# p in three bf16 parts read by TensorE at register addresses, and more rows fetched singly

## The chip, the cores and the metric

The kernel runs on one core of a Trainium2 chip. A core has five engines with a queue of instructions each: TensorE (PE in the profile, its weight loads PEld), VectorE (DVE), ScalarE (ACT), GpSimd (POOL) and SyncE (SP); SP, ACT and POOL also issue DMAs. The metric is the device time of one execution in microseconds.

## The reference

One layer of graph attention over 6250 nodes with 128 features and 206,250 edges (src, dst), then ELU, a residual and a layer norm:

```python
recv, send = edge_index[:, 0], edge_index[:, 1]
n_in, n_out = node[recv], node[send]
wn_out = n_out @ W_lin + b_lin
e_ij = leaky_relu2(jnp.concatenate([n_in, n_out], axis=-1) @ W_att + b_att)
a_ij = (e_ij @ w_alpha)[:, 0]
seg_max = jax.ops.segment_max(a_ij, recv, num_segments=N_NODES)
a_exp = jnp.exp(a_ij - seg_max[recv])
denom = jax.ops.segment_sum(a_exp, recv, num_segments=N_NODES)
alpha = a_exp / jnp.maximum(denom[recv], 1e-12)
n_i = jax.ops.segment_sum(alpha[:, None] * wn_out, recv, num_segments=N_NODES)
x = _layernorm(x + elu(n_i), axis=-1)
```

The product with W_att splits into a part p of the receiver and a part q of the sender, so p, q and v = wn_out are computed once per node and not once per edge.

## The kernel before

**Table.** 49 blocks of 128 nodes are taken in 25 pairs. For each pair PE computes p, q and v (`project`, L921 the f32 product and L922 the bias), ACT copies p into SBUF (`p_all`, L700, f32) and q and v into an outgoing tile (L704), and SP stores the latter to the table `qv_table` in DRAM, one row of 1 KB per node. Before every other pair PE transposes the next x (L910) and ACT copies it (L695). There are two PSUM buffers, so a projection waits for the copies of the pair two before it.

**Sort.** Meanwhile DVE sorts the first set of edges by receiver's block, a bitonic network (L1185, L1186) in runs; between runs PE transposes the keys (L942) and ACT copies them back (L715, L721, L722). Three lists set where on PE and ACT the pairs stand among the runs: `TABLE_BEFORE` ahead of the first turn, `TABLE_BEHIND` (run: pairs) and `TABLE_LAST`.

**Main loop.** The sorted edges are 1660 units of 128 edges, in 415 chunks of 4 units, in four sets; the next set is sorted inside the loop of the one before (same lines). For chunk k:
- POOL gathers q and v of the senders of each unit with one indirect DMA (L666) into a ring of 8 chunks. Every 11th chunk (`ROW_CHUNKS`) has one unit that is not gathered: its 128 rows are fetched by one DMA each, spread over the 11 chunks before, 104 issued by SP (L584) and 24 (`BY_ACT`) by ACT (L810, in `fetch_rows`), with addresses loaded into registers 8 at a time.
- DVE compares each edge's receiver lane with the lanes' numbers: `onehotT` (L1574).
- ACT loads four block numbers packed in a word into its registers (L443) and copies the four blocks of p that the units need to `p_unit` at register addresses (L761, `stage_p`).
- PE, `hidden`: for each unit it transposes the gathered q (L1005) and adds p_unit x onehotT in PSUM (L1007, f32, which takes two passes).
- ACT makes the slope (L768), DVE the leaky relu (L1581), PE the logits with a mask per block (L1017, L1018), DVE the chunk's lows and running peaks (L1588, L1603) and the growth (L1613).
- ACT `weigh` takes four exps (L778), PE transposes the weights (L1025), ACT copies them (L793, `copy_weights`) and turns growth into a shrink factor (L787, `lessen`); PE sums weights x v per unit (L1033) and DVE adds it to the node sums (L1625).

The order in each engine's queue is written out by hand. ACT's step k is weigh(k+2), slope(k+4), copy_weights(k+1), lessen(k+2), stage_p(k+6), fetch_rows(k+6), then side work, such as a count of edges per block in chunks 23 to 71 (L869). PE's is high_sums(k), hidden(k+4), turn_weights(k+1), mask(k+3), low_sums(k+1). Before its loop ACT fetches the rows of the first `ROWS_AHEAD` = 6 chunks.

Of the kernel before, what the change touches and what calls it, by code (L numbers as in the profile page):

```python
# [13 lines left out]
P = 128  # L14
# [6 lines left out]
def gnn_kernel(nc, x, src, dst, w_lin, b_lin, w_att, b_att, w_alpha, out):  # L21
# [83 lines left out]
    ROWS_EACH = 8  # L105
    ROW_CHUNKS = 11
    BY_ACT = 3 * ROWS_EACH
    BY_SP = UNIT - BY_ACT
# [80 lines left out]
    with ExitStack() as ctx:  # L189
        def sb(name, shape, dt):  # L190
            return ctx.enter_context(nc.sbuf_tensor(name, shape, dt))
# [4 lines left out]
        def sem(name):  # L196
            return ctx.enter_context(nc.semaphore(name))
# [18 lines left out]
        pad_rows = sb("pad_rows", [P, R], F32)  # L216
        p_all = sb("p_all", [P, NB * F], F32)
        p_unit = sb("p_unit", [P, 2, CHUNK], F32)
        sums = sb("sums", [P, NB, F + 1], F32)
# [109 lines left out]
        kept_i = kept[:].bitcast(I32)  # L329
        onehotT_b = onehotT[:].bitcast(BF16).rearrange("p r (e h) -> p r e h", h=2)[:, :, :, 1]  # L330
        columns_i = columns[:].bitcast(I32)
# [57 lines left out]
        pqv_ps = sem("pqv_ps")  # L389
        p_ready = sem("p_ready")  # L390
        p_staged = sem("p_staged")
        qv_ready = sem("qv_ready")
# [284 lines left out]
        def _(act):  # L677
# [12 lines left out]
            def copy_xT(q):  # L690
# [4 lines left out]
                a.activation(xT[:, q % 2, 0:n], masked_ps[:, q % 2, 0:n], ACT.Copy).then_inc(xT_ready, 1)  # L695

            def table_pair(g):
                n = min(2, NB - 2 * g)
                act.wait_ge(pqv_ps, g + 1)
                a.activation(p_all[:, 2 * g * F:(2 * g + n) * F].rearrange("p (n f) -> p n f", f=F),  # L700
                             pair_ps[g % 2][:, 0:n, 0:F], ACT.Copy).then_inc(p_ready, 1)
                if g >= 2:
                    act.wait_ge(qv_stored[g % 2], g // 2 * 16)
                a.activation(qv_out[:, g % 2, 0:n, :], pair_ps[g % 2][:, 0:n, F:3 * F], ACT.Copy).then_inc(qv_ready, 1)  # L704
                if g % 2 == 0 and g // 2 + 1 < QUADS:
                    copy_xT(g // 2 + 1)

            copy_xT(0)
            for g in TABLE_BEFORE:
# [39 lines left out]
            for g in TABLE_LAST:  # L749
                table_pair(g)  # L750

            def stage_p(k):

                s, n = place(k)
                if n == 0:
                    act.wait_ge(blk_packed, 4 * (s + 1))
                of = blocks_of(mybir.EngineType.Activation, k, F)
                if k >= 2:
                    act.wait_ge(hidden_done, k - 1)
# [56 lines left out]
            act.wait_ge(pad_rows_stored, 16)  # L816
            act.wait_ge(p_ready, PAIRS)
            for k in range(2):
                stage_p(k)
            for k in range(ROWS_AHEAD):  # L820
                fetch_rows(k)
            for k in range(4):
                if k >= 2:
                    weigh(k - 2)
                slope(k)
                stage_p(k + 2)
                if k >= 2:
                    lessen(k - 2)
            copy_weights(0)

            def step(k):
                if k + 2 < NCH:
                    weigh(k + 2)
                if k + 4 < NCH:
                    slope(k + 4)
                if k + 1 < NCH:
                    copy_weights(k + 1)
                if k + 2 < NCH:
                    lessen(k + 2)
                if k + 6 < NCH:  # L840
                    stage_p(k + 6)
                fetch_rows(k + ROWS_AHEAD)
                besides(k)
# [54 lines left out]
        def _(pe):  # L898
# [26 lines left out]
            def table_pair(g):  # L925
                if g % 2 == 0 and g // 2 + 1 < QUADS:
                    turn_x(g // 2 + 1)
                if g + 1 < PAIRS:
                    project(g + 1)

            turn_x(0)
            project(0)
# [60 lines left out]
            def hidden(k):  # L993

                pe.wait_ge(onehotT_ready, k + 1)
                pe.wait_ge(p_staged, k + 1)
                if k >= 2:
                    pe.wait_ge(leaky_ready, k - 1)
                pe.wait_ge(gathered[k % U], come[k])
                if k in single_no:  # L1000
                    pe.wait_ge(*fetched_in(single_no[k]))
                whole = hidden_ps[:, k % 2, :]
                for c in range(C):
                    unit = slice(c * P, (c + 1) * P)
                    t.matmul(whole[:, unit], rows_at_unit(k, c)[:, 0:F], identf[:], is_transpose=True,  # L1005
                             start=True, stop=False, skip_group_check=True)
                    mm = t.matmul(whole[:, unit], p_unit[:, k % 2, unit], onehotT[:, k % 4, unit],  # L1007
                                  start=False, stop=True, skip_group_check=True)
                mm.then_inc(hidden_done, 1)

            def mask(k):

                pe.wait_ge(leaky_ready, k + 1)
                if k >= 2:
                    pe.wait_ge(weightsT_ready, k - 1)
                whole = masked_ps[:, k % 2, :]
                t.matmul(whole, other[:], onehotT_b[:, k % 4, :], start=True, stop=False)  # L1017
                t.matmul(whole, w_cols[:], leaky[:, k % 2, :], start=False, stop=True).then_inc(masked_done, 1)  # L1018
# [23 lines left out]

            pe.wait_ge(p_ready, PAIRS)
            pe.wait_ge(qv_ready, PAIRS)
# [711 lines left out]
```

## Time and profile before

| | |
|---|---|
| median of 3 runs | 2260.75 us (2259.72 to 2261.03) |
| the profiled execution | 2259.84 us, span 2258.1 us |
| busy in the span | PE 80%, PEld 63%, DVE 82%, ACT 65%, POOL 70% |
| indirect gathers on POOL (L666) | 1623, 958 ns each |

The profile is one execution, read from the hardware's trace. An engine's busy time leaves out what its queue does besides: loads of registers, address arithmetic and the issue of DMAs, which on ACT and SP stand in the timeline as ACTq and SPq. A wait is put down to what ended it; "issue" is idle time in which the engine waited for nothing that the trace shows.

### The profile page before, as it was taken

What the parts mean: (1) busy time and instruction counts of PE and PEld (TensorE: products, weight loads), DVE (VectorE), ACT (ScalarE), POOL (GpSimd) and SP (SyncE); (2) the same over time, 40 slices, a digit from 0 to 9 for tenths busy, and PEclk for the clock granted to TensorE, in tenths of its full rate; (3) what the DMA queues carried; (4) which work ended last, traced back from release to release, by engine and by line L of the source; (5) the groups of instructions that cost most, each with busy time, mean ns of one, the idle gap of its engine ahead of it and who ended that gap; (6) DMA issues with size and microseconds to landing.
All of it is one profiled execution on the core that took longest, in us unless ns stands there. A gap on an engine that the chain in (4) does not pass through costs nothing.

```text
span 2258.1 us, 63519 instructions
## 1 busy us (share of the span) xinstructions
PE 1811.7 (80%) x11705; PEld 1421.1 (63%) x11705; DVE 1855.0 (82%) x5630; ACT 1468.1 (65%) x4913; POOL 1582.8 (70%) x1658
## 2 busy tenths in 40 slices
PE   5648888888988888887888988888889878888870
PEld 2336666666766776666666767666667666666660
DVE  9849988888789889887998998888776667676667
ACT  2326677777666776665666776666666666666665
POOL 2057777777777777777777777777777777777760
PEclk9769999999999999999999999999999999999995
DMA  3134444445444444444444445444454544444431
GB/s 122 56 112 139 136 137 134 135 134 142 131 135 134 135 137 133 136 138 130 135 136 131 130 138 137 138 134 136 133 137 136 138 137 134 138 135 136 136 109 57
DMA packets 168219, 293.30 MB, mean 130 GB/s; under 512 B 41346, under 2 KB 112894, under 8 KB 167825
## 3 DMA queue, kind: packets, MB, share of 16 engines
q0 software_dynamic: 78288, 213.62, 33.2%
q1 hardware_dynamic: 87029, 74.44, 12.1%
q14 instruction: 293, 2.40, 0.3%
q8 instruction: 101, 1.65, 0.3%
q10 hardware_dynamic: 2508, 1.18, 0.2%
HBM read 278.10 MB, written 10.99 MB: 128 GB/s over the span
## 4 chain that ended last, share of the span: by engine, by line
POOL 17%; issue 12%; DVE 9%; PE 8%; DMA 3%; ACT 2%; DVEq 2%; ACTq 1%; POOLq 0%
POOL rows L666 17%; DMA rows<-qv_table,senders 3%; DVE sums L1625 2%; PE turned_ps L1033 2%; PE hidden_ps L1007 2%; DVE leaky L1581 2%; PE masked_ps L1018 2%; DVEq L1625 1%; PE hidden_ps L1005 1%; PE turned_ps L1025 1%; DVEq L443 1%; ACT spare L778 1%; ACTq L810 1%; DVE keys L1186 1%; DVE keys L1185 1%
## 5 line engine op out<-in xcount | busy, mean ns | idle before, releaser
L666 POOL DMA_INDIRECT rows<-qv_table,senders x1623 | 1555.1, 958 | 496.3 <-issue 468.0
L1033 PEld LDWEIGHTS turned_ps<-rows,spare 128*128 128x128 f32 x3246 | 423.2, 191 | 479.7 <-ACT spare L793 368.6
L1625 DVE SCALAR_TENSOR_TENSOR sums<-sums,shrink,turned_ps 128x129 f32 x1660 | 573.2, 345 | 135.8 <-PE turned_ps L1033 59.4
L778 ACT ACTIVATE spare<-masked_ps,peaks 128x128 f32<-128x128 f32 x1660 | 472.0, 368 | 303.6 <-DVE peaks L1603 225.3
L1033 PE MATMUL turned_ps<-rows,spare 128*128 128x129 f32 x3246 | 501.6, 287 | 173.7 <-ACT spare L793 91.2
L1007 PE MATMUL hidden_ps<-onehotT,p_unit 128*128 128x128 f32 x3320 | 591.2, 280 | 0.0
L1005 PE MATMUL hidden_ps<-identf,rows 128*128 128x128 f32 x1623 | 454.6, 280 | 143.9 <-DMA rows<-qv_table,senders 132.9
L1007 PEld LDWEIGHTS hidden_ps<-onehotT,p_unit 128*128 128x128 f32 x3320 | 519.3, 197 | 0.6 <-issue 0.6
L761 ACT ACTIVATE p_unit<-p_all 128x128 f32 x1660 | 410.4, 316 | 106.3 <-issue 83.1
L1588 DVE TENSOR_REDUCE lows<-masked_ps 128x4 f32<-128x512 f32 x415 | 285.2, 687 | 192.5 <-PE masked_ps L1018 191.4
L1018 PE MATMUL masked_ps<-leaky,w_cols 128*128 128x512 f32 x830 | 426.6, 595 | 0.0
L1005 PEld LDWEIGHTS hidden_ps<-identf,rows 128*128 128x128 f32 x1623 | 235.5, 145 | 167.0 <-issue 158.4
L768 ACT ACTIVATE sloped<-hidden_ps 128x512 f32<-128x512 f32 x415 | 252.5, 608 | 120.3 <-PE hidden_ps L1007 118.4
L1574 DVE TENSOR_SCALAR_CACHE_REDUCE onehotT<-lanes_all,part_f 128x512 f32<-128x512 bf16 x415 | 307.1, 740 | 16.5 <-DMA lanes_all<-lane_list 16.5
L1581 DVE TENSOR_TENSOR leaky<-hidden_ps,sloped 128x512 f32<-128x512 f32 x415 | 283.9, 684 | 0.5
L793 ACT ACTIVATE spare<-turned_ps 128x512 f32<-128x512 f32 x415 | 254.6, 613 | 3.9 <-PE turned_ps L1025 3.7
L1025 PE MATMUL turned_ps<-identf,spare 128*128 128x128 f32 x1660 | 253.9, 276 | 0.0
L1185 DVE TENSOR_TENSOR keys<-keys 128x256 f32<-128x256 f32 (+2 forms) x501 | 196.1, 391 | 19.4 <-ACT keys L715 7.4
L1025 PEld LDWEIGHTS turned_ps<-identf,spare 128*128 128x128 f32 x1660 | 199.9, 144 | 0.5 <-issue 0.5
L1186 DVE TENSOR_TENSOR keys<-keys 128x256 f32<-128x256 f32 (+2 forms) x501 | 194.5, 388 | 0.0
L1018 PEld LDWEIGHTS masked_ps<-leaky,w_cols 128*128 128x128 f32 x830 | 159.7, 192 | 21.2
L1017 PE MATMUL masked_ps<-onehotT,other 128*128 128x512 bf16 x415 | 163.9, 395 | 6.0 <-DVE leaky L1581 5.8
(203 smaller groups left out, 920.3 us busy)
## 6 DMA issues: line engine op xcount, KB each, us to landing
single_rows<-qv_table SPq DMA_DIRECT2D x3848, 1.0 KB
lanes_all<-lane_list SPq DMA_DIRECT2D x415, 128.0 KB
rows<-qv_table,senders POOLq DMA_INDIRECT x1623
single_rows<-qv_table ACTq DMA_DIRECT2D x888, 1.0 KB
qv_table<-rows SPq DMA_DIRECT2D x24, 256.0 KB, 2.2
out<-x_sb SPq DMA_DIRECT2D x1, 1344.0 KB
out<-x_sb SPq DMA_DIRECT2D x1, 896.0 KB
kept<-windows SPq DMA_DIRECT2D x3, 208.0 KB
```

Source lines behind the costliest of these rows:

```text
L666: g.indirect_dma_start(out=rows[:, k % U, c, 0:R], out_offset=None, in_=table, in_offset=bass.IndirectOffsetOnAxis(ap=senders[:, s % 2, c ...
L761: last = a.activation(p_unit[:, k % 2, c * F:(c + 1) * F], p_all[:, bass.ds(of[c], F)], ACT.Copy)
L778: last = a.activation(weightsT[:, k % 2, unit], masked_ps[:, k % 2, unit], ACT.Exp, bias=peaks[:, at + 2 * n:at + 2 * n + 1])
L1005: t.matmul(whole[:, unit], rows_at_unit(k, c)[:, 0:F], identf[:], is_transpose=True, start=True, stop=False, skip_group_check=True)
L1007: mm = t.matmul(whole[:, unit], p_unit[:, k % 2, unit], onehotT[:, k % 4, unit], start=False, stop=True, skip_group_check=True)
L1018: t.matmul(whole, w_cols[:], leaky[:, k % 2, :], start=False, stop=True).then_inc(masked_done, 1)
L1025: mm = t.transpose(weights_ps[:, c * P:(c + 1) * P], weightsT[:, k % 2, c * P:(c + 1) * P], identf[:])
L1033: mm = t.matmul(unit_sums_ps[:, c, :], weights[:, k % 2, c * P:(c + 1) * P], rows_at_unit(k, c)[:, F:PLACE], start=True, stop=True)
L1574: v.tensor_scalar(onehotT[:, k % 4, :], lanes_all[:, k % LANE_RING, :], part_f[:], None, ALU.is_equal, ALU.add, accum_out=lane_counts[:, k ...
L1581: v.tensor_tensor(leaky[:, k % 2, :], hidden_ps[:, k % 2, :], sloped[:, k % 2, :], ALU.max).then_inc(leaky_ready, 1)
L1588: v.tensor_reduce(lows_at[:, n * PER:(n + 1) * PER, 1], masked_ps[:, k % 2, :].rearrange("p (i e) -> p i e", i=PER), AX_X, ALU.max, negate ...
L1625: v.scalar_tensor_tensor(out=at, in0=at, scalar=shrink[:, k % 4, i:i + 1], in1=unit_sums_ps[:, i, :], op0=ALU.mult, op1=ALU.add).then_inc( ...
```

## The change

p is kept as three bf16 tiles, `p_high`, `p_middle` and `p_low`, whose sum is p. ACT copies the high part from PSUM, PE takes it off again there (a product of minus the identity with the part, added to the PSUM tile), ACT copies what is left as the middle part, and so once more. `p_all`, `p_unit` and ACT's `stage_p` are gone: PE loads the packed block numbers itself and multiplies the three parts at register addresses with onehotT, which is now bf16 too. A unit of every 8th chunk is fetched by rows instead of every 11th, with 56 of its 128 rows issued by ACT and 72 by SP, so 7 and 9 a chunk. The pairs of the table stand elsewhere among the runs of the sort.

```diff
-    ROW_CHUNKS = 11
-    BY_ACT = 3 * ROWS_EACH
+    ROW_CHUNKS = 8
+    BY_ACT = 7 * ROWS_EACH
...
-    TABLE_BEFORE = [0, 1, 2, 3, 4, 5, 6, 7, 8]
-    TABLE_BEHIND = {1: [9, 10], 3: [11, 12], 5: [13, 14], 6: [15], 7: [16, 17], 8: [18, 19], 9: [20, 21], 10: [22, 23]}
+    TABLE_BEFORE = [0, 1, 2, 3, 4, 5, 6, 7]
+    TABLE_BEHIND = {1: [8, 9], 3: [10, 11], 5: [12, 13], 6: [14], 7: [15, 16, 17], 8: [18], 9: [19, 20, 21], 10: [22, 23]}
...
-        onehotT = sb("onehotT", [P, 4, CHUNK], F32)
+        onehotT = sb("onehotT", [P, 4, CHUNK], BF16)
...
+            def part_of_p(g, part):
+                n = min(2, NB - 2 * g)
+                return a.activation(part[:, 2 * g * F:(2 * g + n) * F].rearrange("p (n f) -> p n f", f=F),
+                                    pair_ps[g % 2][:, 0:n, 0:F], ACT.Copy)
...
             def table_pair(g):
                 n = min(2, NB - 2 * g)
                 act.wait_ge(pqv_ps, g + 1)
-                a.activation(p_all[:, 2 * g * F:(2 * g + n) * F].rearrange("p (n f) -> p n f", f=F),
-                             pair_ps[g % 2][:, 0:n, 0:F], ACT.Copy).then_inc(p_ready, 1)
+                part_of_p(g, p_high).then_inc(high_ready, 1)
                 if g >= 2:
                     act.wait_ge(qv_stored[g % 2], g // 2 * 16)
                 a.activation(qv_out[:, g % 2, 0:n, :], pair_ps[g % 2][:, 0:n, F:3 * F], ACT.Copy).then_inc(qv_ready, 1)
+                if g >= 1:
+                    low_part(g - 1)
                 if g % 2 == 0 and g // 2 + 1 < QUADS:
                     copy_xT(g // 2 + 1)
-
+                act.wait_ge(high_off, g + 1)
+                part_of_p(g, p_middle).then_inc(middle_ready, 1)
...
-            def stage_p(k):
...
-                for c in range(C):
-                    last = a.activation(p_unit[:, k % 2, c * F:(c + 1) * F], p_all[:, bass.ds(of[c], F)], ACT.Copy)
-                last.then_inc(p_staged, 1)
...
             def project(g):
                 pe.wait_ge(xT_ready, g // 2 + 1)
                 if g >= 2:
-                    pe.wait_ge(p_ready, g - 1)
+                    pe.wait_ge(low_ready, g - 1)
                     pe.wait_ge(qv_ready, g - 1)
...
+            def take_off(g, part):
+                for n in range(min(2, NB - 2 * g)):
+                    mm = t.matmul(pair_ps[g % 2][:, n, 0:F], minus[:], part[:, (2 * g + n) * F:(2 * g + n + 1) * F],
+                                  start=False, stop=True, skip_group_check=True)
+                return mm
+
             def table_pair(g):
                 if g % 2 == 0 and g // 2 + 1 < QUADS:
                     turn_x(g // 2 + 1)
+                pe.wait_ge(high_ready, g + 1)
+                pe.wait_ge(qv_ready, g + 1)
+                take_off(g, p_high).then_inc(high_off, 1)
                 if g + 1 < PAIRS:
                     project(g + 1)
-
+                pe.wait_ge(middle_ready, g + 1)
+                take_off(g, p_middle).then_inc(middle_off, 1)
...
             def hidden(k):
 
+                s, n = place(k)
+                if n == 0:
+                    pe.wait_ge(blk_packed, 4 * (s + 1))
+                of = blocks_of(mybir.EngineType.PE, k, F)
                 pe.wait_ge(onehotT_ready, k + 1)
-                pe.wait_ge(p_staged, k + 1)
...
-                    mm = t.matmul(whole[:, unit], p_unit[:, k % 2, unit], onehotT[:, k % 4, unit],
-                                  start=False, stop=True, skip_group_check=True)
+                    for part in (p_high, p_middle, p_low):
+                        mm = t.matmul(whole[:, unit], part[:, bass.ds(of[c], F)], onehotT[:, k % 4, unit],
+                                      start=False, stop=part is p_low, skip_group_check=True)
```

ACT's queue in one step of the loop, before (`single_at` holds the addresses of the rows, `packed` the block numbers):

```order
L778 ACTIVATE spare<-masked_ps,peaks 128x128 [waits new_low_ready,weights_done]
L778 ACTIVATE spare<-masked_ps,peaks 128x128 x3
L768 ACTIVATE sloped<-hidden_ps 128x512 [waits leaky_ready,hidden_done]
L793 ACTIVATE spare<-turned_ps 128x512 [waits high_sums_done,weights_done]
L787 ACTIVATE shrink<-growth 128x4 [waits sums_ready,growth_ready]
L443 TENSOR_LOAD packed
L761 REGISTER_ALU [waits hidden_done]
L761 ISA
L761 ACTIVATE p_unit<-p_all 128x128
```

Behind these rows three more copies with two REGISTER_ALU and an ISA ahead of each follow, and then two DMAs of rows (L810). The same step of ACT's queue after the change, whole:

```order
L786 ACTIVATE spare<-masked_ps,peaks 128x128 [waits new_low_ready,weights_done]
L786 ACTIVATE spare<-masked_ps,peaks 128x128 x3
L776 ACTIVATE sloped<-hidden_ps 128x512 [waits leaky_ready,hidden_done]
L801 ACTIVATE spare<-turned_ps 128x512 [waits high_sums_done,weights_done]
L795 ACTIVATE shrink<-growth 128x4 [waits sums_ready,growth_ready]
L818 DMA single_rows<-qv_table 1x1024 x3
L470 TENSOR_LOAD single_at
L818 DMA single_rows<-qv_table 1x1024 x4
```

The load of block numbers, the register work and the four copies are gone; seven rows stand in their place, with a load of eight addresses among them in seven of eight steps.

PE's queue in `hidden`, two units of the four, before:

```order
L1005 MATMUL hidden_ps<-identf,rows 128x128 [waits leaky_ready,gathered7,p_staged,onehotT_ready]
L1007 MATMUL hidden_ps<-onehotT,p_unit 128x128
L1005 MATMUL hidden_ps<-identf,rows 128x128
L1007 MATMUL hidden_ps<-onehotT,p_unit 128x128
```

And after, the load and the first unit, with the start of the second:

```order
L448 TENSOR_LOAD packed
L1022 MATMUL hidden_ps<-identf,rows 128x128 [waits gathered3,leaky_ready,onehotT_ready]
L1025 REGISTER_ALU
L1025 ISA
L1025 MATMUL hidden_ps<-onehotT,p_high 128x128
L1025 REGISTER_ALU
L1025 MATMUL hidden_ps<-onehotT,p_middle 128x128
L1025 REGISTER_ALU
L1025 MATMUL hidden_ps<-onehotT,p_low 128x128
L1022 MATMUL hidden_ps<-identf,rows 128x128
L1025 REGISTER_ALU x2
L1025 ISA
```

The wait for ACT's staging is gone; a load a chunk and four or five register instructions a unit have come to PE's own queue.

PE's queue in the table, one pair and the projection of the next, before (`hidden_ps` and `turned_ps` are the two PSUM buffers that the pairs use in turn):

```order
L910 MATMUL masked_ps<-identf,x_sb 128x128 x3
L921 MATMUL turned_ps<-w,rows 128x384 [waits qv_ready,p_ready,xT_ready]
L922 MATMUL turned_ps<-bias_parts,onesb 128x384
L921 MATMUL turned_ps<-w,rows 128x384
L922 MATMUL turned_ps<-bias_parts,onesb 128x384
L921 MATMUL hidden_ps<-w,rows 128x384 [waits qv_ready,p_ready,xT_ready]
```

And after:

```order
L912 MATMUL masked_ps<-identf,x_sb 128x128 x3
L929 MATMUL hidden_ps<-p_high,minus 128x128 [waits qv_ready,high_ready]
L929 MATMUL hidden_ps<-p_high,minus 128x128
L923 MATMUL turned_ps<-w,rows 128x384 [waits qv_ready,low_ready,xT_ready]
L924 MATMUL turned_ps<-bias_parts,onesb 128x384
L923 MATMUL turned_ps<-w,rows 128x384
L924 MATMUL turned_ps<-bias_parts,onesb 128x384
L929 MATMUL hidden_ps<-p_middle,minus 128x128 [waits middle_ready]
L929 MATMUL hidden_ps<-p_middle,minus 128x128
```

Ahead of a projection PE now waits for ACT's copies of the pair just before it, where it waited for those of the pair two before.

## Rows read from the trace of the kernel before

**Rows 1.** Sums of waits: engine, line, waited for, us, times, longest.

```profile
POOL rows L666 <- issue: 468.0, 1535, 0.3
ACT spare L778 <- DVE peaks L1603: 225.3, 260, 6.4
```

**Rows 2.** Costliest groups: count, busy us, mean ns, idle before and its releaser.

```profile
L666 POOL DMA_INDIRECT rows<-qv_table,senders x1623 | 1555.1, 958 | 496.3 <-issue 468.0
...
L1007 PE MATMUL hidden_ps<-onehotT,p_unit 128*128 128x128 f32 x3320 | 591.2, 280 | 0.0
```

**Rows 3.** Timeline, POOL: start, us, line, count, idle before and its releaser.

```profile
131.25 0.98 POOL L666 DMA_INDIRECT rows<-qv_table,senders  x1 [0.30 <-issue]
...
1206.24 0.95 POOL L666 DMA_INDIRECT rows<-qv_table,senders  x1 [0.30 <-issue]
```

**Rows 4.** Timeline, ACT and its DMA queue (ACTq), late in the loop.

```profile
1838.32 1.14 ACT L778 ACTIVATE spare<-masked_ps,peaks 128x128 f32<-128x128 f32 x4 [0.74 <-DVE peaks L1603]
...
1840.45 0.99 ACT L761 ACTIVATE p_unit<-p_all 128x128 f32 x4
1841.21 0.79 ACTq L810 DMA_DIRECT2D single_rows<-qv_table  x2
1842.10 0.62 ACT L778 ACTIVATE spare<-masked_ps,peaks 128x128 f32<-128x128 f32 x2 [0.66 <-DVE peaks L1603]
...
1855.39 1.14 ACTq L810 DMA_DIRECT2D single_rows<-qv_table  x3
...
1868.09 1.82 ACTq L810 DMA_DIRECT2D single_rows<-qv_table  x2
```

**Rows 5.** Line 443 by itself: count, ns least/median/most, first and last start.

```profile
L443 ACTq TENSOR_LOAD <-packed x415: 274/462/533, 138.6 to 2186.6; - x139
```

**Rows 6.** Timeline, ACT and ACTq, in the stretch that counts edges.

```profile
361.89 0.72 ACT L869 ACTIVATE counting<-last_blocks,thresholds 128x512 bf16<-128x512 bf16 x1 [1.39 <-issue]
...
365.13 0.47 ACTq L810 DMA_DIRECT2D single_rows<-qv_table  x1
365.25 0.33 ACT L761 ACTIVATE p_unit<-p_all 128x128 f32 x1
...
366.02 0.72 ACT L869 ACTIVATE counting<-last_blocks,thresholds 128x512 bf16<-128x512 bf16 x1 [0.44 <-issue]
```

**Rows 7.** Stretches: us, busy (count) of PE, PEld, DVE, ACT, POOL; PEclk, DMA.

```profile
84.00:97.00 13.00, 9.00 (x32) 5.26 (x31) 11.91 (x52) 4.66 (x13) 0.00 (x0) 0.76 0.18 62
...
270.00:515.00 245.00, 206.90 (x1376) 160.92 (x1377) 213.00 (x635) 192.07 (x652) 186.17 (x194) 1.00 0.49 135
```

**Rows 8.** Timeline, ACT's first rows and its first slope.

```profile
141.81 5.82 ACTq L810 DMA_DIRECT2D single_rows<-qv_table  x13
147.68 0.60 ACT L768 ACTIVATE sloped<-hidden_ps 128x512 f32<-128x512 f32 x1 [6.23 <-PE hidden_ps L1007]
```

**Rows 9.** Timeline, the last pairs ahead of the sort's first turn.

```profile
42.88 0.38 ACT L700 ACTIVATE p_all<-hidden_ps 128x256 f32<-128x256 f32 x1 [0.74 <-PE hidden_ps L922]
...
43.16 0.59 ACT L704 ACTIVATE rows<-hidden_ps 128x512 f32<-128x512 f32 x1
...
43.76 0.33 PE L922 MATMUL turned_ps<-bias_parts,onesb 128*128 128x384 bf16 x1
...
44.57 0.33 PE L922 MATMUL turned_ps<-bias_parts,onesb 128*128 128x384 bf16 x1
...
46.83 0.29 DVE L1185 TENSOR_TENSOR keys<-keys 128x128 f32<-128x128 f32 x1 [0.61 <-ACT keys L722]
```

**Rows 10.** Timeline, PE and DVE at turns of the keys behind later runs.

```profile
66.29 0.44 PE L942 MATMUL turned_ps<-identf,keys 128*128 128x128 f32 x2 [1.18 <-DVE keys L1186]
...
91.11 0.69 PE L942 MATMUL turned_ps<-identf,keys 128*128 128x128 f32 x2 [3.23 <-DVE keys L1186]
...
100.06 0.43 DVE L1185 TENSOR_TENSOR keys<-keys 128x256 f32<-128x256 f32 x1 [2.50 <-ACT keys L715]
```

**Rows 11.** Timeline, SP's queue late in the loop.

```profile
1836.38 4.06 SPq L584 DMA_DIRECT2D single_rows<-qv_table  x10
```

More of the change, by code:

```diff
@@ L216, in gnn_kernel @@
         pad_rows = sb("pad_rows", [P, R], F32)
-        p_all = sb("p_all", [P, NB * F], F32)
-        p_unit = sb("p_unit", [P, 2, CHUNK], F32)
+        p_high = sb("p_high", [P, NB * F], BF16)
+        p_middle = sb("p_middle", [P, NB * F], BF16)
+        p_low = sb("p_low", [P, NB * F], BF16)
+        minus = sb("minus", [P, P], BF16)
         sums = sb("sums", [P, NB, F + 1], F32)
@@ L389, in gnn_kernel @@
         pqv_ps = sem("pqv_ps")
-        p_ready = sem("p_ready")
-        p_staged = sem("p_staged")
+        minus_ready = sem("minus_ready")
+        high_ready = sem("high_ready")
+        middle_ready = sem("middle_ready")
+        low_ready = sem("low_ready")
+        high_off = sem("high_off")
+        middle_off = sem("middle_off")
         qv_ready = sem("qv_ready")
@@ L695, in copy_xT, with low_part @@
                 a.activation(xT[:, q % 2, 0:n], masked_ps[:, q % 2, 0:n], ACT.Copy).then_inc(xT_ready, 1)
+            def part_of_p(g, part):
+                n = min(2, NB - 2 * g)
+                return a.activation(part[:, 2 * g * F:(2 * g + n) * F].rearrange("p (n f) -> p n f", f=F),
+                                    pair_ps[g % 2][:, 0:n, 0:F], ACT.Copy)
+            def low_part(g):
+                act.wait_ge(middle_off, g + 1)
+                part_of_p(g, p_low).then_inc(low_ready, 1)
             def table_pair(g):
@@ L704, in table_pair @@
                 a.activation(qv_out[:, g % 2, 0:n, :], pair_ps[g % 2][:, 0:n, F:3 * F], ACT.Copy).then_inc(qv_ready, 1)
+                if g >= 1:
+                    low_part(g - 1)
                 if g % 2 == 0 and g // 2 + 1 < QUADS:
                     copy_xT(g // 2 + 1)
+                act.wait_ge(high_off, g + 1)
+                part_of_p(g, p_middle).then_inc(middle_ready, 1)
+            act.wait_ge(consts, 6)
+            a.activation(minus[:], identf[:], ACT.Copy, scale=-1.0).then_inc(minus_ready, 1)
             copy_xT(0)
@@ L750, in _ @@
                 table_pair(g)
-            def stage_p(k):
[L754 to L759, printed above, removed]
-                for c in range(C):
-                    last = a.activation(p_unit[:, k % 2, c * F:(c + 1) * F], p_all[:, bass.ds(of[c], F)], ACT.Copy)
-                last.then_inc(p_staged, 1)
+            low_part(PAIRS - 1)
             def slope(k):
@@ L816, in _ @@
             act.wait_ge(pad_rows_stored, 16)
-            act.wait_ge(p_ready, PAIRS)
-            for k in range(2):
-                stage_p(k)
             for k in range(ROWS_AHEAD):
@@ L825, in _ @@
                 slope(k)
-                stage_p(k + 2)
                 if k >= 2:
@@ L839, in step @@
                     lessen(k + 2)
-                if k + 6 < NCH:
-                    stage_p(k + 6)
                 fetch_rows(k + ROWS_AHEAD)
@@ L1016, in mask @@
                 whole = masked_ps[:, k % 2, :]
-                t.matmul(whole, other[:], onehotT_b[:, k % 4, :], start=True, stop=False)
+                t.matmul(whole, other[:], onehotT[:, k % 4, :], start=True, stop=False)
                 t.matmul(whole, w_cols[:], leaky[:, k % 2, :], start=False, stop=True).then_inc(masked_done, 1)
@@ L1041, in high_sums @@
                 unit_sums(k, PER // 2, PER, high_sums_done)
-            pe.wait_ge(p_ready, PAIRS)
+            pe.wait_ge(low_ready, PAIRS)
             pe.wait_ge(qv_ready, PAIRS)
```

2 lines of the change are left out of this document (1 added, 1 removed).

## The prediction

> **What bounds the kernel now.** I read the sums of waits first, then the costliest groups, then one step of each engine in order of time. The whole main loop hangs on POOL: it issues 1623 indirect gathers [rows 2], and its only large idle time is its own 0.30 us of issue ahead of each, 468 us in 1535 gaps [rows 1]. A gather takes 0.95 us, and with the 0.30 ahead 1.25 [rows 3]; a chunk has 1623/415 = 3.91 gathers, which makes 4.89 us, and in the counting stretch 194 gathers in 245 us make 1.263 us each, 4.94 us a chunk [rows 7]. The other engines have room, ACT the least to judge by its queue: one of its steps runs from the first weigh at 1838.32 to the next at 1842.10, 3.78 us [rows 4], and the rest of a POOL step it spends waiting for DVE's peaks, 225 us in all [rows 1]. The rows fetched singly are the one thing with which gathers are bought off POOL, and they are paid for on the queues of SP and ACT.
>
> Before the loop, whose first gather is at 131.25 us [rows 3], stand table and first sort, in which PE, ACT and DVE share the work: DVE sorts, PE and ACT make the table in the gaps, and DVE waits where PE comes late.
>
> **The change part by part.**
>
> Gathers. 415/8 instead of 415/11 chunks have a unit fetched by rows, so there are 1609 gathers instead of 1623, as the code counts them: 14 x 1.25 = 17.5 us less for POOL. This is the whole gain that is to be had while POOL sets the pace, -17.5 us, or 4.85 us a chunk.
>
> ACT's step in the loop. The p copies go: before each chunk's rows ACT loads the packed blocks (0.46 us, [rows 5]), works out addresses and starts four copies; from the first copy to the first row DMA 0.76 us pass (1840.45 to 1841.21, [rows 4]). With some 0.13 us of register arithmetic ahead, which no row shows (estimate), the queue is relieved of 1.35 us a chunk. What comes is rows: 7 a chunk instead of 2.1. Two rows take 0.79 us and three 1.14 us [rows 4], so 0.35 us for each further one and 2.54 us for seven; a group of two with an address load inside takes 1.82 us [rows 4], 1.03 us more, while a load ahead of the group costs less (the first DMA is slow anyway). There is a load in 7 of 8 chunks, so X = 2.54 + 7/8 x (0.6 to 1.03) = 3.1 to 3.4 us; I take 3.3. The rest of ACT's step is 3.78 - 1.35 - 0.85 = 1.6 us. Its step after: 1.6 + 3.3 = 4.9 us, against POOL's 4.85. So outside the counting stretch two queues are equally long, and each waits for the other's late steps now and then. Of POOL's gain there (366 chunks x 0.042 = 15.4 us) I take half, -8 us; the bounds are -15 and, if ACT's step comes out 0.1 us longer than POOL's old one, +37.
>
> The counting stretch (49 chunks with one more ACTIVATE and its read on ACT). A step with nothing waited for lasts from 361.89 to 366.02, 4.13 us [rows 6]. Less 1.35 and 0.7 for two rows that leaves 2.05; with X it is 5.35 us against 4.94: 49 x 0.4 = 20 us. The queue can start rows while ACTIVATEs already issued still run, as the row of 365.13 ahead of the last copy at 365.25 shows [rows 6], so less is possible; I take +14, between 0 and +22.
>
> ACT's start. Its first six chunks of rows stand ahead of its first slope: 13 rows with one load took 5.82 us, and slope began at 147.68, right behind [rows 8]. Now there are 42 rows and 6 loads: 0.79 + 40 x 0.35 + 6 x 0.85 = 20 us. The copies that delayed the rows before go, so slope begins at some 158 to 160 rather than 147.7. POOL has a ring of eight chunks, 39 us of gathers, before it needs chunk 0's rows back; much of the lateness is taken up by that. I take +6, between 0 and +12.
>
> Table, before the sort's first run ends. Per pair ACT made two copies (0.28 us apart, then 0.59) beside PE's next projection, whose halves are 0.81 us apart (43.76, 44.57, [rows 9]); PE paced it at 2 x 0.81 and half a group of transposes, 1.84 us. Now PE waits for both copies of a pair before it takes the high part off, and behind that wait stand the next projection and the keys' own transposes: 0.87 of ACT, about 0.2 for two small products, 1.62 for the projection, 0.2 for transposes, 0.1 for hand-overs make 3.0 us. Eight pairs x 3.0 = 24.0 against nine x 1.84 = 16.6: PE is free 7.4 us later. Before, it was free at 44.9 and DVE's next run waited 0.61 us for it at 46.83 [rows 9], so there is no cover for that: +7.
>
> Table, behind the runs. With two pairs behind run 7 PE had 3.23 us to spare before the keys came at 91.11, and behind run 9 as much; behind run 8 it was late, and DVE waited 2.50 us at 100.06 [rows 10]. Three pairs at 3.0 to 3.3 instead of two at 1.9 are 5.5 us more, 2.3 late behind runs 7 and 9 each; run 8, with one pair for two, gives back some 1.5; runs 1, 3 and 5 go from 3.8 to 6.1 with 1.2 to spare (66.29, [rows 10]), some 1 us late each. Together +6. With the +7 the loop starts 13 us later, between +5 (hand-overs that overlap better, ACT less late) and +22.
>
> PE's clock decides where between these. In the stretch of runs 7 and 8 the granted clock was 0.76 on average [rows 7]: a mixture of 1.2 and 2.4 GHz, with PE idle between the runs, while the dense first pairs take 0.81 us a half. The change cuts that dense stretch into 2 us of PE and 1 us of waiting for ACT. The Trainium skill (TensorE: Matmul & The Clock Gate, What's actually happening) calls the throttled clock the default that activity releases, which speaks against this change: by that rule the first pairs could fall to 1.2 GHz. If they stay at 2.4 GHz the sum above holds; at 1.2 GHz each pair takes 1.6 us more, 13 us over eight. I take the upper clock, since even that stretch of long pauses kept 0.76; the lower one is inside the range.
>
> PE in the loop. Each unit's f32 product (two passes, 280 ns each, 3320 in all, [rows 2]) becomes three bf16 ones, but the block's address is now reckoned on PE's own queue: a load a chunk and five register instructions a unit, ahead of matmuls that DVE's onehot and the gathers release. No row shows these on PE; on ACT a load is 0.46 us [rows 5] and one unit's copy with its three register instructions 0.23 to 0.25 us. The lower bound is a gain of 0.2 us a chunk (shorter products), the upper a loss of 0.46 + 4 x 0.38 - 1.1 = 0.9 us. PE's busy share of the counting stretch is 207 of 245 us [rows 7], 0.77 us a chunk free, so I cost it at nothing and keep the upper end as a rival.
>
> SP, DVE. SP has 9 rows a chunk instead of 9.5, at ten in 4.06 us [rows 11]; that cannot hurt. onehot in bf16 instead of f32: I see no row that makes it faster, 0.
>
> Sum: -8 + 14 + 6 + 13 = +25 us on the profiled execution's 2259.84, 2285 us; it lies 0.9 below the median of the runs, 2260.75, which is nothing here.
>
> **The rivals.**
>
> B: POOL keeps the pace everywhere, since ACT's queue runs ahead and hides the rows in the counting stretch too. For it: the row that started before a copy [rows 6], and ACT's 225 us of waiting [rows 1]. Against it: 4.9 against 4.85. Then -17.5 + 13 + 0 to 6 = -4.5 to +1.5, 2255 to 2261 us.
>
> E, faster: as B, and the table's waits lie beside other work so that the loop starts at most 5 us late. For it: 3.2 us to spare behind two of the runs [rows 10]. Against it: the 0.61 us at 46.83 shows no cover at the end of the first run. It decides if the pair cycle is below 2.4 us. -17.5 + 5 = -12.5, 2247 us.
>
> C: rows cost ACT more. SP, which issues densely, takes 0.41 us a row with its loads [rows 11]; if ACT's rows cost 0.41 beside its loads, X is 3.65 and ACT's step 5.25 in the whole loop and 5.7 in counting, against 4.89 and 4.94 before: 366 x 0.36 + 49 x 0.76 = 169 at the most; half of that, with the queue running ahead, and 19 for start and table are +104, 2364 us. The Trainium skill (Perfetto Trace Analysis, DMA Instruction: HWDGE) says the block that generates descriptors is locked for one DMA at a time and shared by two issuing engines; by that ACT and SP would slow each other. Here the row DMAs of ACT are 0.23 us alone and twice that at the head of a group, beside an SP that issues nearly all the time, so the trace has that cost in it already.
>
> D: PE's register work is not hidden: 0.9 us of loss against 0.77 free, 0.15 a chunk more than POOL's old step: 415 x 0.15 + 19 = +81, 2341 us. For it speaks that every product's address now comes from the same queue just ahead of it, against it the free 0.77.
>
> **How the numbers follow.** Forecast A 0.42 (2265 to 2310), B 0.22, E 0.14, C 0.12, D 0.10. What can be told from no change is 0.2%, 4.5 us, here 2256.2 to 2265.3. Faster: E 0.14 and a third of B, 0.21. Same: the rest of B and A's low end, 0.18. Slower: 0.61. The range runs from the middle of E, 2247, to 2345, which takes in A with its bounds and most of D, and leaves out half of E, 0.07, most of C, 0.10, and a little of D, 0.03.
>
> **What would show it.** First gather at 144 rather than 131.25 us (right from 136 to 153); DVE waits of some 7 us at the end of the first run and 2 us behind runs 7 and 9. On ACT no waits for peaks of any size left, and groups of seven row DMAs of 2.5 us, 3.1 to 3.6 with a load. In the counting stretch gathers 1.35 us apart on average instead of 1.263, with POOL waiting for PE to free the ring. If POOL's idle time is issue alone all along, B or E is right; if the steps of the last 600 us are over 5.1 us, C (ACT's queue full) or D (hidden's matmuls late with their inputs there). A first gather before 136 us would break the table's part, steps of 4.9 us in the counting stretch ACT's part.

## The result and the profile after

The changed kernel takes 2343.4 us (median of 5 runs, 2340.9 to 2345.0) against 2261.0: a ratio of 1.036, interval 1.035 to 1.037, so 82 us or 3.6% slower. The sign was forecast, the size not: 2285 was the single figure, a loss of 25 us, and the measured loss is over three times that.

The share of the chain that ended last, by engine, of the profile after:

```profile
ACTq 26%; issue 13%; ACT 12%; PE 12%; DVE 6%; POOL 3%; DVEq 1%; DMA 1%; POOLq 0%
```

ACT's own DMA queue leads: 19% of the span is the issue of single rows (L818), 6% the loads of their addresses (L470). Sums of waits of the profile after, read as in [rows 1]:

```profile
ACT spare L786 <- issue: 579.0, 199, 3.7
POOL rows L671 <- issue: 472.9, 1487, 2.1
ACT spare L786 <- DVE peaks L1621: 232.1, 116, 3.7
POOL rows L671 <- PE turned_ps L1051: 102.5, 122, 5.1
```

POOL now waits 102 us for PE to free its ring, and weigh stands 579 us behind something that is no other engine: the row DMAs ahead of it on its queue. In the counting stretch 189 gathers fit in 260 us, 1.376 us each where it was 1.263 [rows 7] (1.35 was forecast):

```profile
286.00:546.00 260.00, 232.06 (x1522) 163.90 (x1546) 212.17 (x627) 146.15 (x450) 179.73 (x189) 0.99 0.47 125
```

Where the 81 us between the two profiled spans lie follows from the starts of two events, the first gather and DVE's reduction of a chunk's lows (L1588 before, L1606 after):

| part | before | after | difference, us |
|---|---|---|---|
| first gather, at | 131.3 us | 145.8 us | +14.5 |
| from there to the first lows | 27.2 us | 30.0 us | +2.8 |
| chunks 0 to 21, a chunk | 4.80 | 4.88 | +2 |
| 21 to 73 (counting, sort) | 4.97 | 5.34 | +19 |
| 73 to 90 | 4.84 | 5.28 | +7 |
| 90 to 164 (sort) | 4.98 | 5.29 | +23 |
| 164 to 179 | 5.24 | 5.11 | -2 |
| 179 to 286 (sort) | 4.95 | 5.16 | +22 |
| 286 to 414 (no sort) | 4.88 | 4.82 | -8 |

The last row is what was hoped for of 14 fewer gathers. Most of the loss, 64 us, is in the three long stretches beside which the next set is sorted. The 7 us of chunks 73 to 90, only four of which have a sort beside them, are something else: there the kernel before made up for a late chunk, with steps of 3.91 us on average in chunks 83 to 89, and the changed kernel, whose ACT has seven rows to issue in each step, takes 4.70. One step beside the sort on ACT, timeline of the profile after, in the columns of [rows 4]:

```profile
1215.03 0.62 ACT L801 ACTIVATE spare<-turned_ps 128x512 f32<-128x512 f32 x1
1215.50 0.23 ACTq L818 DMA_DIRECT2D single_rows<-qv_table  x1
1215.51 0.24 ACT L795 ACTIVATE shrink<-growth 128x4 f32<-128x4 f32 x1
1215.83 2.94 ACTq L818 DMA_DIRECT2D single_rows<-qv_table  x6
1218.88 1.14 ACT L786 ACTIVATE spare<-masked_ps,peaks 128x128 f32<-128x128 f32 x4 [3.13 <-issue]
```

and DVE's timeline beside it:

```profile
1214.65 0.41 DVE L1204 TENSOR_TENSOR keys<-keys 91x256 f32<-91x256 f32 x1
1214.99 0.34 DVE L1643 SCALAR_TENSOR_TENSOR sums<-sums,shrink,turned_ps 128x129 f32 x1
1215.25 0.15 DVE L1631 TENSOR_TENSOR growth<-peaks 128x4 f32<-128x4 f32 x1
...
1217.10 0.23 DVE L1621 TENSOR_TENSOR_SCAN peaks<-fresh,peaks,lows 128x8 f32<-128x8 bf16 x1
```

lessen needs DVE's growth, which comes behind the sort's four instructions and a sum; it is ready at 1215.40, the rows start at 1215.50 and end at 1218.77, and only then does the next weigh start, though its peaks were there at 1217.33. The group is 3.3 us, as forecast; that it starts late was not. This step is no exception: in chunks 179 to 286 the first row starts within 0.2 us of the end of growth in 69% of the steps, in chunks 286 to 395, without a sort, in 2%.

The unsorted end shows the same queue without that delay: growth is there at 1905.16, 0.8 us ahead of the first row, rows begin 1.3 us behind weigh's start, and the step is 4.70 us:

```profile
1904.63 1.14 ACT L786 ACTIVATE spare<-masked_ps,peaks 128x128 f32<-128x128 f32 x4 [2.34 <-DVE peaks L1621]
...
1905.94 0.23 ACTq L818 DMA_DIRECT2D single_rows<-qv_table  x1
...
1909.33 0.62 ACT L786 ACTIVATE spare<-masked_ps,peaks 128x128 f32<-128x128 f32 x2 [2.49 <-DVE peaks L1621]
```

(Where a wait is named DVE's peaks here, the peaks are 0.9 to 1.0 us old; the row issue came last.)

On PE, hidden reads its parts with register work between. Its timeline after, the third unit of a chunk:

```profile
1202.48 0.28 PE L1022 MATMUL hidden_ps<-identf,rows 128*128 128x128 f32 x1
1202.73 0.23 PE L1025 MATMUL hidden_ps<-onehotT,p_high 128*128 128x128 bf16 x1
1202.85 0.22 PE L1025 MATMUL hidden_ps<-onehotT,p_middle 128*128 128x128 bf16 x1
1202.96 0.22 PE L1025 MATMUL hidden_ps<-onehotT,p_low 128*128 128x128 bf16 x1
1203.02 0.28 PE L1022 MATMUL hidden_ps<-identf,rows 128*128 128x128 f32 x1
```

The same of the kernel before:

```profile
1202.75 0.27 PE L1005 MATMUL hidden_ps<-identf,rows 128*128 128x128 f32 x1
1202.86 0.39 PE L1007 MATMUL hidden_ps<-onehotT,p_unit 128*128 128x128 f32 x2
1203.08 0.27 PE L1005 MATMUL hidden_ps<-identf,rows 128*128 128x128 f32 x1
```

Here a unit takes 0.54 us from transpose to transpose, where it took 0.33 (the medians of all are 0.53 and 0.33). From the first to the last matmul's start, the median of hidden is 1.89 us (1.74 to 2.10 for the middle half) after and 1.22 before. The load itself is short:

```profile
L448 PEldq TENSOR_LOAD <-packed x415: 295/301/994, 154.4 to 2273.5; - x139
```

The table, ACT's timeline with two pairs' first copies, and DVE's waits at the turns of the keys:

```profile
39.89 0.38 ACT L704 ACTIVATE p_high<-hidden_ps 128x256 bf16<-128x256 f32 x1 [1.43 <-PE hidden_ps L924]
...
43.03 0.38 ACT L704 ACTIVATE p_high<-turned_ps 128x256 bf16<-128x256 f32 x1 [1.22 <-PE turned_ps L924]
```

```profile
53.27 0.29 DVE L1203 TENSOR_TENSOR keys<-keys 128x128 f32<-128x128 f32 x1 [7.38 <-ACT keys L741]
...
89.75 0.29 DVE L1203 TENSOR_TENSOR keys<-keys 128x128 f32<-128x128 f32 x1 [2.37 <-ACT keys L741]
...
104.92 0.29 DVE L1203 TENSOR_TENSOR keys<-keys 128x128 f32<-128x128 f32 x1 [2.30 <-ACT keys L741]
...
122.36 0.29 DVE L1203 TENSOR_TENSOR keys<-keys 128x128 f32<-128x128 f32 x1 [3.50 <-ACT keys L741]
```

A pair's cycle is 3.14 us (3.0 forecast), DVE waits 7.38 us at the first run's end where it waited 0.61 [rows 9]. TensorE's clock stayed at its upper level there:

```profile
30.00:55.00 25.00, 18.89 (x98) 10.73 (x96) 16.24 (x59) 13.36 (x38) 0.96 (x4) 1.00 0.22 76
```

Ahead of its first slope ACT issues all 42 rows, 19.8 us (20 forecast, [rows 8]):

```profile
152.19 19.79 ACTq L818 DMA_DIRECT2D single_rows<-qv_table  x42
172.02 1.09 ACT L776 ACTIVATE sloped<-hidden_ps 128x512 f32<-128x512 f32 x2 [34.65 <-issue]
```

The theory formed from this (theory 1): the loop's loss is a ring through three engines, growth (DVE), lessen and the rows (ACT), weigh, PE's part of the step, the sums on DVE, growth again. Whatever lengthens a link while the sort is beside it lengthens the step. The rivals: ACT's queue is just full, whatever the order (theory 2); PE's register work alone (theory 3); the table alone.

### The profile page after: what moved, and what is told of

Read it like the earlier page. It is cut to its first block, busy times and chain, and to the rows that moved or that the text cites. A ratio compares the mean times of both kernels' runs of the same rounds, so it can differ in the third digit from the quotient of the medians.

```text
span 2339.2 us, 72025 instructions
## 1 busy us (share of the span) xinstructions
PE 2057.4 (88%) x13256; PEld 1444.1 (62%) x13463; DVE 1865.6 (80%) x5630; ACT 1079.2 (46%) x3304; POOL 1569.5 (67%) x1644
## 4 chain that ended last, share of the span: by engine, by line
ACTq 26%; issue 13%; ACT 12%; PE 12%; DVE 6%; POOL 3%; DVEq 1%; DMA 1%; POOLq 0%
ACTq L818 19%; ACT spare L786 7%; ACTq L470 6%; PE hidden_ps L1025 4%; PE turned_ps L1051 4%; POOL rows L671 3%; ACT spare L801 2%; ACT sloped L776 2%; PE turned_ps L1043 2%; PE hidden_ps L1022 1%; DVE sums L1643 1%; PE masked_ps L1036 1%; DVE leaky L1599 1%; DVEq L1643 1%; DMA rows<-qv_table,senders 1%
## 5 line engine op out<-in xcount | busy, mean ns | idle before, releaser
L1051 PEld LDWEIGHTS turned_ps<-rows,spare 128*128 128x128 f32 x3218 | 412.4, 192 | 424.8 <-ACT spare L801 378.8
L1051 PE MATMUL turned_ps<-rows,spare 128*128 128x129 f32 x3218 | 489.9, 288 | 106.6 <-ACT spare L801 75.2
L1606 DVE TENSOR_REDUCE lows<-masked_ps 128x4 f32<-128x512 f32 x415 | 285.3, 687 | 192.9 <-PE masked_ps L1036 192.4
L1025 PE MATMUL hidden_ps<-onehotT,p_high 128*128 128x128 bf16 x1660 | 378.0, 228 | 8.7 <-issue 0.3
L1025 PE MATMUL hidden_ps<-onehotT,p_low 128*128 128x128 bf16 x1660 | 364.1, 219 | 1.1
L1025 PE MATMUL hidden_ps<-onehotT,p_middle 128*128 128x128 bf16 x1660 | 364.1, 219 | 1.1
L1592 DVE TENSOR_SCALAR_CACHE_REDUCE onehotT<-lanes_all,part_f 128x512 bf16<-128x512 bf16 x415 | 306.5, 739 | 11.8 <-DMA lanes_all<-lane_list 11.8
L1025 PEld LDWEIGHTS hidden_ps<-onehotT,p_high 128*128 x1660 | 161.7, 97 | 191.9 <-issue 169.6
L1043 PEld LDWEIGHTS turned_ps<-identf,spare 128*128 128x128 f32 x1660 | 177.1, 142 | 15.1 <-issue 0.9
L1025 PEld LDWEIGHTS hidden_ps<-onehotT,p_low 128*128 x1660 | 161.1, 97 | 31.8 <-issue 3.6
```

The lines of the kernel that those rows point to most:

```text
L1025: mm = t.matmul(whole[:, unit], part[:, bass.ds(of[c], F)], onehotT[:, k % 4, unit], start=False, stop=part is p_low, skip_group_check=True)
L1043: mm = t.transpose(weights_ps[:, c * P:(c + 1) * P], weightsT[:, k % 2, c * P:(c + 1) * P], identf[:])
L1051: mm = t.matmul(unit_sums_ps[:, c, :], weights[:, k % 2, c * P:(c + 1) * P], rows_at_unit(k, c)[:, F:PLACE], start=True, stop=True)
L1592: v.tensor_scalar(onehotT[:, k % 4, :], lanes_all[:, k % LANE_RING, :], part_f[:], None, ALU.is_equal, ALU.add, accum_out=lane_counts[:, k ...
```

## The experiments

All ratios are against the kernel before on the same chip; it took 2260.6 to 2260.9 us there.

**Rows ahead of lessen.** In ACT's step:

```diff
+                fetch_rows(k + ROWS_AHEAD)
                 if k + 2 < NCH:
                     lessen(k + 2)
-                fetch_rows(k + ROWS_AHEAD)
```

> The changed kernel with ACT's rows put ahead of lessen in its step, so that they no longer stand behind the wait for DVE's growth; the same rows, the same p. Theory 1 (lateness comes from rows that start only when growth is there): in the stretches that sort inside the loop a step falls from 5.1 to POOL's 4.85 us, in the counting stretch from 5.35 to about 5.2; 2343 falls by 45 to 55, to 2288 to 2298 us, and the idle time of ACT ahead of lessen for growth is gone. Theory 2 (ACT's queue is simply full with seven rows and the rest, whatever the order): within 10 us of 2343. Theory 3 (PE's register work): within 10 us of 2343.

2319.0 us, 1.026 (1.024 to 1.027): 24 us back, half of what theory 1 said, more than theory 2 or 3. (The first gather came at 142.7 us in this trace, with the same table as after, so some 21 us of it are the loop's.) The rows now start before growth (1216.36 where growth ends at 1216.84), so that wait is gone from the rows' path:

```profile
1216.36 0.23 ACTq L818 DMA_DIRECT2D single_rows<-qv_table  x1
1216.52 0.62 ACT L801 ACTIVATE spare<-turned_ps 128x512 f32<-128x512 f32 x1
1216.69 2.95 ACTq L818 DMA_DIRECT2D single_rows<-qv_table  x6
1219.74 0.21 ACT L795 ACTIVATE shrink<-growth 128x4 f32<-128x4 f32 x1 [2.61 <-DVE sums L1643]
```

**Growth ahead of the sort** (and of the sum behind it), the same link cut on the other engine. In DVE's step:

```diff
+                if k + 2 < NCH:
+                    grow(k + 2)
                 besides(k)
                 add_sums(k, 2, of)
-                if k + 2 < NCH:
-                    grow(k + 2)
```

> The changed kernel with DVE's growth moved ahead of the sort's instructions in DVE's step, behind leaky; ACT's order unchanged. Theory 1: growth comes some 1.0 us behind peaks instead of 2.9, lessen no longer waits for it, and the sorting stretches fall to POOL's 4.85 us: 2285 to 2300. Theory 2 (queue full): within 10 us of 2343.

2313.9 us, 1.023 (1.021 to 1.025): 30 us back; chunks 179 to 286 fall from 5.16 to 5.06, not to 4.85. ACT's queue is full in the step shown, from one weigh to the next, though growth is there at 1205.90, 2 us before lessen (1207.93). DVE's line and ACT's timeline:

```profile
1205.75 0.15 DVE L1631 TENSOR_TENSOR growth<-peaks 128x4 f32<-128x4 f32 x1
```

```profile
1205.94 1.15 ACT L786 ACTIVATE spare<-masked_ps,peaks 128x128 f32<-128x128 f32 x4 [2.84 <-issue]
...
1207.58 0.56 ACTq L818 DMA_DIRECT2D single_rows<-qv_table  x2
...
1208.23 2.66 ACTq L818 DMA_DIRECT2D single_rows<-qv_table  x5
1211.00 0.63 ACT L786 ACTIVATE spare<-masked_ps,peaks 128x128 f32<-128x128 f32 x2 [2.84 <-issue]
```

So the wait and the fulness of the queue both count.

**The old rows with the three parts.**

```diff
-    ROW_CHUNKS = 8
-    BY_ACT = 7 * ROWS_EACH
+    ROW_CHUNKS = 11
+    BY_ACT = 3 * ROWS_EACH
```

> The changed kernel with the old rows: every 11th chunk, 24 by ACT and 104 by SP. p stays in three parts. Theory 1 (ACT's rows are what is late in the loop): ACT's step is some 2.7 us, never late, POOL paces at 4.89 us a chunk; 2261 + 14.5 for the table - 0 to 10 = 2265 to 2276 us. Theory 3 (PE's register work is what is late): steps stay above 5 us, 2325 or more.

2274.5 us, 1.006 (1.004 to 1.008), as theory 1 had it. The loop is as before (4.95 us in chunks 179 to 286, 4.88 at the end), ACT waits 550 us for peaks, and only the first gather, at 147.6 us, is late. So the parts cost the table's 14 us, and PE's longer hidden (its median is 2.11 us here) costs nothing as long as ACT has room; 69 us of the 82 need the new rows. (Here, too, the first row starts within 0.2 us of growth in 58% of the steps of chunks 179 to 286; a group of 0.64 us behind that wait makes nothing late.)

**The new rows alone**, the lines above in the kernel before.

> The kernel before with the new rows alone (every 8th chunk, 56 by ACT, 72 by SP); p in f32, copied by ACT as before, table as before. Theory 1: rows and copies stand one behind the other on ACT's queue, 1.55 + 1.35 + 3.3 = 6.2 us a step and more where growth is waited for: 2261 + 415 x 1.3 to 1.6 = 2800 to 2925 us. Theory 2': the queue runs ahead and hides much of it: 2500 or less.

2672 us, 1.182 (1.178 to 1.186): the direction, but between the two cases. In the first of two successive steps on ACT the rows end 0.10 us ahead of the next weigh, and the second is longer still:

```profile
1199.76 1.15 ACT L778 ACTIVATE spare<-masked_ps,peaks 128x128 f32<-128x128 f32 x4 [3.08 <-issue]
...
1202.87 2.08 ACTq L810 DMA_DIRECT2D single_rows<-qv_table  x6
1205.05 1.15 ACT L778 ACTIVATE spare<-masked_ps,peaks 128x128 f32<-128x128 f32 x4 [2.27 <-issue]
...
1207.94 3.56 ACTq L810 DMA_DIRECT2D single_rows<-qv_table  x7
```

Chunks took 5.4 us at the end and 6.0 to 6.4 while sorting. So the copies that the change removes seem to have been worth less of ACT's queue than the 1.35 us reckoned: at the end 5.42 - 4.82 = 0.6 us, where the 4.82 is POOL's pace and so 0.6 a lower bound, and 0.9 to 1.1 while sorting, where ACT's queue is full in most steps of both. One reason is in the trace: rows start beside ACTIVATEs that wait in line (a row at 1201.54, the first copy at 1201.83). And not all of the 2672 need be ACT's queue: PE's granted clock was 0.90 from 140 to 800 us of this run and 0.97 from 131 to 800 us of the kernel before; what that cost was not measured.

**Six rows a chunk on ACT**, `BY_ACT = 6 * ROWS_EACH`, ten on SP.

> The changed kernel with 48 of the 128 rows on ACT and 80 on SP, 6 and 10 a chunk; nothing else. ACT's row group is then about 2.85 us instead of 3.3. If both the wait for growth and the length of the group count (they stand one behind the other), sorting stretches fall from 5.2 to about 5.0 and the total to 2290 to 2310 us. If only the fulness of ACT's queue counts, its step is 1.5 + 2.85 + 0.1 = 4.45, POOL paces everywhere, and the total is 2260 to 2268. If SP were the limit with its tenth row (4.1 us and 0.35 for the lanes), 2343 or more.

2288.2 us, 1.011 (1.010 to 1.013): 55 us for one row fewer in a step, just under the 2290 to 2310 of both causes together. It is the largest single lever: chunks 179 to 286 fall from 5.16 to 4.98, those from 21 to 73 from 5.34 to 5.16, so the length of the group counts, but not alone. No harm from SP's tenth row shows: the chunks at the end take 4.79 us.

**Both**: growth ahead of the sort and six rows.

> Both at once: DVE's growth ahead of the sort's instructions, and 6 rows a chunk on ACT. Then neither the wait nor the length of ACT's step is above POOL's 4.85 us, and only the table and the 14 gathers are left of the change: 2261 + 14.5 + 2 - 17.5 = 2260, 2256 to 2268 us. If something else holds the sorting stretches at 5.05 us (PE's register work, contention of DMAs), 2285 or more.

2275.8 us, 1.007 (1.005 to 1.008): between the two cases. Chunks 179 to 286 are back at 4.95 and the end is at 4.79, but chunks 21 to 164 stay at 5.06 to 5.15, so something else is late there.

**No register work on PE**: the products read parts of p at addresses known when the program is built. This leaves out which block a unit needs, and with it the load and the register arithmetic.

```diff
-                        mm = t.matmul(whole[:, unit], part[:, bass.ds(of[c], F)], onehotT[:, k % 4, unit],
+                        mm = t.matmul(whole[:, unit], part[:, (k * C + c) // 34 * F:((k * C + c) // 34 + 1) * F], onehotT[:, k % 4, unit],
```

> The changed kernel with the blocks of p read by PE at addresses fixed when the program is built, so that PE has no load and no register arithmetic in the loop (left out: which block of p a unit needs). The same products, the same ACT. If ACT's chain alone (growth, rows, weigh) holds the loop, 2343 within 10 us. If PE's register work is part of it, 2300 to 2325.

2309.9 us, 1.021 (1.020 to 1.023): 34 us back. hidden's median falls from 1.89 to 1.07 us between its first and last start, shorter than the 1.22 before the change: the three bf16 products are cheaper than one f32 product, and the register work eats that and 0.67 us more.

The same edit on top of growth_first_six_rows:

> growth_first_six_rows with p's addresses fixed in the same way (left out: which block of p a unit needs). There ACT is no longer late, and chunks 21 to 164 still take 5.06 us instead of 4.97 as before. If PE's register work holds them there, 16 us of 2276 go: 2257 to 2266. If it is something else, 2272 to 2280.

2260.4 us, 1.000 (0.999 to 1.001): 15 us, as the first case said. Chunks 21 to 73 take 4.79 us now (5.06), those from 90 to 164 4.95 (5.06). That names the third link. With all three taken out the loop gains some 14 us on the kernel before, which just pay for the table.

**The parts made by GpSimd**, to spare PE's wait for ACT in the table: ACT copies p in f32 as before, GpSimd makes each pair's parts.

```diff
+                for part in (p_high, p_middle):
+                    g.tensor_copy(part[:, at], whole).then_inc(parts_done, 1)
...
+                    last = g.tensor_tensor(out_at, whole, part[:, at], ALU.subtract)
```

> As the run before, and the three parts of p are made by GpSimd (idle in the table stage) out of an f32 copy by ACT, so that PE and ACT make the table as in the kernel before, with its lists of pairs. If the table's loss is PE's wait for ACT, the first gather is at 131 again and the time 14 below the run before: 2243 to 2254 us. If GpSimd's 100 instructions slow DVE's sort beside them (memory port), or come too late for the first gather, 2258 or more.

> The changed kernel with the old rows (every 11th chunk, 24 by ACT) and the parts made by GpSimd, table as in the kernel before; DVE's order unchanged. It leaves of the change only p's reading on PE in the loop. If the 14 us of parts_with_old_rows are the table's, 2256 to 2264 us; if they are PE's in the loop, 2272 or more.

2286.2 us, 1.011 (1.010 to 1.013), and 2287.7 us, 1.012 (1.011 to 1.014): 10 and 13 us worse than with PE. The second was to tell the table from PE's reading of p, and its time alone, above 2272, would blame PE; the trace does not. The first gather comes at 157.5 and 157.8 us. In the second DVE waits for its keys for no more than 1.2 us at a time, but its sort ends at 141.96 us where it ended at 115.60 in the kernel before: it is slow beside GpSimd, as two timelines show:

```profile
38.85 0.50 DVE L1195 TENSOR_TENSOR keys<-keys 128x256 f32<-128x256 f32 x1
39.28 0.89 DVE L1196 TENSOR_TENSOR keys<-keys 128x256 f32<-128x256 f32 x1
```

```profile
39.16 0.73 POOL L656 TENSOR_TENSOR rows<-rows,p_high 128x256 f32<-128x256 f32 x1
```

The loop of the second is as with the old rows (4.96 in chunks 179 to 286), so the whole of the loss is ahead of the loop.

**The table's pairs spread**: from growth_first_six_rows,

```diff
-    TABLE_BEFORE = [0, 1, 2, 3, 4, 5, 6, 7]
-    TABLE_BEHIND = {1: [8, 9], 3: [10, 11], 5: [12, 13], 6: [14], 7: [15, 16, 17], 8: [18], 9: [19, 20, 21], 10: [22, 23]}
-    TABLE_LAST = [24]
+    TABLE_BEFORE = [0, 1, 2, 3, 4, 5]
+    TABLE_BEHIND = {1: [6, 7], 3: [8, 9], 5: [10, 11], 6: [12], 7: [13, 14], 8: [15], 9: [16, 17], 10: [18, 19, 20]}
+    TABLE_LAST = [21, 22, 23, 24]
```

> growth_first_six_rows with two pairs fewer ahead of the sort's first turn (6), two pairs instead of three behind runs 7 and 9, three behind run 10 and four behind the last. If the table's loss is only PE's lateness at the turns, DVE's wait at the first run's end falls from 7.4 to about 1.5 us, those behind 7 and 9 to none, the first gather comes at 135 to 139 instead of 145 us and the time is 2266 to 2270. If the pairs at the end stand in the way of the last steps of the sort, 2275 or more.

2264.3 us, 1.002 (1.001 to 1.003), a little better than forecast: DVE's first wait falls from 7.4 to 1.70 us and the first gather comes at 139.7 us in place of 145.3. Only 8 us are left of the table's 14.

**And two parts**: the middle part is the last; hidden has two bf16 products a unit.

> table_spread with p in two bf16 parts instead of three (left out: the low part, some 2 to the power of -17 of p). A pair's cycle loses one round between PE and ACT, hidden loses a quarter of its products: if PE's hidden holds the sorting stretches, 2252 to 2260 us; if not, within 4 us of table_spread.

2255.4 us, 0.998 (0.997 to 0.999): the only version faster than both kernels, by 5.5 us, at the price of p's low part. Chunks 21 to 164 take 4.93 us where three parts took 5.06: the gain is in the loop. Its first gather, at 143.8, came later than table_spread's, with shorter work per pair; why is open. (In eight traces with the table of the changed kernel it came between 142.7 and 147.6 us, so a few us between two traces may mean nothing.)

## Why the prediction was wrong

- POOL's gain (-17.5 at most): right where nothing else is late; the last 128 chunks gave 8 us, 0.06 a chunk for the 0.04 reckoned.
- The table (+13): right. +14.5 in the trace, a pair's cycle 3.14 for 3.0, DVE's waits 7.4 for 7, and behind the later runs 2.4, 2.3 and 3.5, the last not forecast; 14 us in the time of the run with the old rows.
- The clock: the upper level was taken, and 1.00 was granted; the throttled default that the Trainium skill (TensorE: Matmul & The Clock Gate, What's actually happening) describes did not come back in those pairs, for all their pauses.
- ACT's start: 19.8 us of rows for 20; its cost 2.8 for 6.
- The counting stretch (+14): +19 in chunks 21 to 73, inside its bounds, but partly by luck: there, too, 63% of the steps have their first row within 0.2 us of growth, and sorting chunks that count nothing lost 0.2 to 0.3 us each against 0.37 here. What counting itself cost was not separated.
- **ACT's step outside the counting stretch (-8): this is the step that failed.** It came to about +45. The prediction set the sum of ACT's queue, 4.9 us, beside POOL's 4.85 and took the rest of a step to be waiting that could be filled. The size of that sum was near (4.70 us in the step shown of the unsorted end), and the bound of +37 for a longer step had no wait in it. (The 0.13 us of register arithmetic in it, an estimate, is 0.2 us in the trace of the kernel before, from the end of the load at 1840.24 to the first copy at 1840.45.) But the rows stand behind lessen, and lessen behind growth, which DVE gives 2.9 us after peaks while it sorts. Work put behind such a wait doesn't fill it; it is added to the chain that leads to the next weigh. Both orders that take the wait off that path gave back 24 and 30 us, one row fewer 55.
- **PE in the loop (0): sized wrongly too.** The upper bound, 0.9 us, was near what the trace shows (0.67 more between first and last start, though a load on PE takes 0.30 us and not 0.46), but it was priced against PE's free time alone. It costs 34 us with the new rows and none with the old: idle time on PE isn't idle time in the chain of waits.
- Of the rivals, C named ACT's queue for the whole loop, but by dearer rows; a group cost 3.3 us as in the forecast itself. D's 2341 us is near by its number only: PE's register work without the new rows cost nothing in the loop. (Nor do its 0.9 us of loss and 0.77 free give 0.15 a chunk; they leave 0.13.)

What stays open: the three cuts give 30, 55 and 34 us singly and 83 together. That the single gains add up to more fits one ring that they share, but also a floor, POOL's pace, below which no cut can help; the ring as a whole is argued from these sums, and how much of it each link holds in a given chunk wasn't measured.

## What to carry to other kernels

Before work is moved into an engine's idle time, see which wait it will stand behind: an engine whose queue has room on average (ACT's step of 3.78 us in POOL's 4.89) can have none at the place where the work goes in. Follow the waits once round (here DVE, ACT, PE, DVE) and price every added instruction on it, also those on engines with room. And take a change of several parts apart on the chip: here the parts, the rows and the order each had its own price.

## What was not expected of the hardware

- DVE's sort instructions took 0.50 and 0.89 us beside GpSimd's tensor instructions (the two shown), where the same shapes took 0.42 without. The Trainium skill (SBUF — State Buffer, Who interferes with whom) says that a VectorE instruction with two inputs from SBUF contends with GpSimd's reads; the trace agrees, and it cost 26 us: with the table's lists of the kernel before, the first gather came at 157.8 instead of 131.3 us.
- Register arithmetic ahead of matmuls can cost as much as the matmuls: with it a unit of hidden takes 0.53 us in the median, and all four 1.89; without it and its load a unit takes 0.28 and all four 1.07 us.
- Three bf16 products with one transpose a unit (1.07 us a chunk from first to last start, at fixed addresses) are faster than an f32 product with it (1.22).
